# A middle stage in groups of four tiles: centred contexts, gathers ahead, inverse roots on ScalarE

## The reference, cut to what matters

```python
x = x + cross_attention_16_heads(layernorm(x), ctx)     # first stage
x = x + ffn_16_experts_capacity_256(layernorm(x))       # expert loop; its gather ends in the middle stage
# third layer (middle stage): ctx is 77 x 128 per tile, used as key and as value
scores = einsum('bqd,bkd->bqk', layernorm(x), ctx) * 128 ** -0.5
scores = where(tril, scores, -inf)
x = x + einsum('bqk,bkd->bqd', softmax(scores), ctx)
# fourth layer (product-key stage) starts from layernorm(x)
x = x + product_key_experts(layernorm(x)) + dense(layernorm(x))

def layernorm(x): return (x - mean(x)) / sqrt(var(x) + 1e-5)
```

## Time and profile before

| | us |
|---|---|
| median of three runs (lowest, highest) | 562.79 (561.74, 563.52) |
| the profiled execution's own time | 563.48 |
| its span, first to last instruction | 561.6 |
| VectorE's last copy of the expert loop starts | 182.49 |
| first maxima of the product-key stage start | 276.47 |
| first weighing on GpSimd (L485) starts | 292.48 |
| busy over the span: PE, DVE, ACT, POOL | 415.8, 387.1, 336.9, 357.5 |

### The profile page before, as it was taken

One profiled execution on the slowest core, in us unless ns is written; L12 is line 12 of the kernel. 1 busy time (PEld: TensorE's weight loads), 2 busy tenths in 40 slices (PEclk: granted clock), 3 DMA queues, 4 the chain that ended last, 5 costly groups with the idle time before them and its releaser, 6 DMA issues.

```text
span 561.6 us, 9520 instructions
## 1 busy us (share of the span) xinstructions
PE 415.8 (74%) x2518; PEld 347.8 (62%) x2518; DVE 387.1 (69%) x1668; ACT 336.9 (60%) x614; POOL 357.5 (64%) x256
## 2 busy tenths in 40 slices
PE   4959877169999034768857787888897778779864
PEld 2757766148999024657636675777676556667754
DVE  3558767102232125977789999999999999999980
ACT  2354553211222033565448888899888899888885
POOL 5227777710000547742249988888988888998883
PEclk9788698559999555555768999888989999998899
DMA  7980001016663101100000000000000000000000
GB/s 204 323 228 25 24 29 39 28 57 195 195 195 107 44 23 38 39 28 0 4 6 11 20 14 14 19 9 19 19 19 9 19 9 19 19 19 9 19 5 15
DMA packets 42415, 29.68 MB, mean 53 GB/s; under 512 B 4155, under 2 KB 38555, under 8 KB 42395
## 3 DMA queue, kind: packets, MB, share of 16 engines
q1 hardware_dynamic: 38539, 22.85, 13.9%
q0 software_dynamic: 2624, 6.30, 3.3%
q10 hardware_dynamic: 1232, 0.31, 0.3%
HBM read 18.95 MB, written 8.39 MB: 49 GB/s over the span
## 4 chain that ended last, share of the span: by engine, by line
DVE 23%; POOL 20%; PE 16%; ACT 12%; issue 7%; DMA 2%; POOLq 1%; DVEq 1%; ACTq 0%; SPq 0%
POOL arena_sb L485 13%; DVE picked_sb L1346 9%; ACT arena_sb L680 6%; PE bank L880 6%; PE bank L890 5%; ACT L680 3%; POOL yg_sb L448 3%; DVE bank L1308 2%; DVE first_sb L1305 2%; POOL slots L416 1%; PE bank L934 1%; POOL rstd_sb L366 1%; DVE bn_sb L1052 1%; DVE best_sb L1334 1%; POOLq L79 1%
## 5 line engine op out<-in xcount | busy, mean ns | idle before, releaser
L485 POOL TENSOR_TENSOR arena_sb<-arena_sb,picked_sb 128x2192 f32<-128x2192 f32 x32 | 154.4, 4847 | 30.8 <-DVE picked_sb L1346 23.7
L1346 DVE SCALAR_TENSOR_TENSOR picked_sb<-arena_sb,best_sb,bank 128x36 f32<-128x36 f32 (+1 forms) x256 | 107.8, 494 | 1.2
L990 PE MATMUL bank<-ident_sb,arena_sb 128*128 128x128 f32 (+1 forms) x512 | 71.8, 300 | 36.0 <-DVE arena_sb L1359 33.0
L990 PEld LDWEIGHTS bank<-ident_sb,arena_sb 128*128 128x128 f32 (+1 forms) x512 | 65.2, 166 | 41.2 <-issue 28.9
L477 POOL TENSOR_TENSOR arena_sb<-near_sb,sim_y_sb 128x1536 f32<-128x1536 f32 x32 | 87.7, 2762 | 1.4 <-DVE near_sb L1313 1.4
L680 ACT ACTIVATE arena_sb<-arena_sb,bsum_sb 128x548 f32<-128x548 f32 x128 | 85.7, 740 | 1.2 <-POOL arena_sb L485 0.8
L674 ACT ACTIVATE arena_sb<-arena_sb 128x2192 f32<-128x2192 f32 x32 | 65.3, 2041 | 0.2
L511 ACT ACTIVATE xn_sb<-x_all_sb,nb_sb,rstd_sb 128x128 f32<-128x128 f32 (+1 forms) x64 | 25.5, 480 | 38.2 <-POOL nb_sb L367 29.9
L981 PE MATMUL bank<-w_down_t_sb,h_sb 128*128 128x128 f32 x256 | 35.6, 284 | 15.8 <-DVE x_all_sb L1365 15.1
L445 POOL CAST made_row_sb<-gather_row_sb 128x4 uint32<-128x4 f32 (+1 forms) x8 | 1.5, 188 | 71.2 <-DMA made<-arena_sb 70.8
L981 PEld LDWEIGHTS bank<-w_down_t_sb,h_sb 128*128 128x128 f32 x256 | 32.0, 196 | 19.3 <-issue 19.3
(11 more groups left out here) (167 smaller groups left out, 928.1 us busy)
## 6 DMA issues: line engine op xcount, KB each, us to landing
w_sb<-w SPq DMA_DIRECT2D x32, 256.0 KB, 3.2
x_all_sb<-x SPq DMA_DIRECT2D x8, 256.0 KB, 2.9
slots<-arena_sb POOLq DMA_DIRECT2D x4, 512.0 KB, 8.3
arena_sb<-slots SPq DMA_DIRECT2D x16, 128.0 KB, 3.0
made<-arena_sb SPq DMA_DIRECT2D x16, 128.0 KB, 1.9
xt_sb<-x_t_sb SPq DMA_DIRECT2D x32, 64.0 KB, 1.8
out<-x_all_sb SPq DMA_DIRECT2D x32, 64.0 KB, 1.6
ctx_t_sb<-ctx_t SPq DMA_DIRECT2D x8, 154.0 KB, 3.6
```

Source lines behind the costliest of these rows:

```text
L485: pool.tensor_tensor(pp[p][:, :, :], pp[p][:, :, :], picked[p][:, :, :], ALU.mult).then_inc(weighed, 1)
L990: ins = pe.matmul(bank[4 * p][0:n, c * P:(c + 1) * P], pp[p][:, h, c * P:c * P + n], ident[:, :], is_transpose=True, start=h == 0, stop=h ...
L1346: ins = dve.scalar_tensor_tensor(out=picked[p][:, h, lo:hi], in0=vv[p][:, h, lo:hi], scalar=best[p][:, h, TOP - 1:TOP], in1=scores, op0=AL ...
```

## The change

The middle stage is unrolled and goes by groups of four tiles instead of pairs of groups; every small buffer of it has two copies, one per parity of the group.

1. Gathers: one cast turns all 32 columns of row numbers into integers, right behind the last scatter. The gathers go to `made_x`, a buffer for all 32 tiles laid over the memory of `picked`. Sixteen are issued at once, then four behind the small operations (`biases3`) of each of the groups 0 to 3.
2. Centring: the transposed contexts are multiplied with a centring matrix (identity less 1/128) in five matmuls of up to 512 columns between the first stage and the expert loop, and ScalarE copies the results over `ctx_t`. A token's mean then adds nothing to its scores, so the raw tile is transposed, and its inverse deviation becomes the scale of the exponential. ScalarE's normalisation ahead of the scores is gone, and the maximum is taken of unscaled scores and multiplied by the scale afterwards (`biases`).
3. Roots: ScalarE computes the inverse root as exp(-1/2 ln(v + eps)), for the second norm of 128 v, which takes in the factor 128 ** -0.5. A set of activation functions is named ahead of the stage.
4. The normalisation for the last stage moves from VectorE to ScalarE, with its bias made by GpSimd from the root.
5. The last group is finished inside the start of the product-key stage: ScalarE's `roots3`, `last_tokens` and `last_tokens_out` stand between `similarities(0, 1)` and `hidden(0, 0)`, TensorE's `last_tokens_t` behind `up(FIRST, 1)`. VectorE has nothing of it.
6. Transposed last tokens use the banks of the attended values; TensorE waits for the last maximum ahead of the first keys. SyncE's first `load_d` waits for one group's tokens, not for a pair's.

```diff
+            pool.tensor_copy(made_row[:, :], gather_row[:, :]).then_inc(made_row_ready, 1)
+            def gathers(g):
+                for n in range(g * BT, g * BT + BT):
+                    pool.indirect_dma_start(out=made_x[:, n, :], out_offset=None, in_=a["made"],
+                                            in_offset=bass.IndirectOffsetOnAxis(ap=made_row[:, n:n + 1], axis=0)
+                                            ).then_inc(gathered[g], 16)
+            def biases3(g):
+                p = g % 2
+                pool.wait_ge(croot3_ready, g + 1)
+                if g >= 2:
+                    pool.wait_ge(cxh_ready, g - 1)
+                step(pool.tensor_tensor(cnb[p][:, :], cmv3[p][:, :, 0], crstd[p][:, :], ALU.mult))
+                pool.tensor_scalar(cnb[p][:, :], cnb[p][:, :], -1.0, None, ALU.mult).then_inc(crstd3_ready, 1)
...
+            hold(pool, made_row_ready, 1)
+            gathers(0)
+            gathers(1)
+            gathers(2)
+            gathers(3)
+            for g in range(NB):
+                biases3(g)
+                if g + 4 < NB:
+                    gathers(g + 4)
```

ScalarE, centring and the middle stage:

```diff
+            for n, (lo, hi) in enumerate(pieces):
+                act.wait_ge(cc_mm, n + 1)
+                copy(cc_ready, ctx_row[:, lo:hi], bank[(0, 2, 3, 4, 6)[n]][:, 0:hi - lo])
...
+            def roots2(g):
+                p = g % 2
+                act.wait_ge(cstat2_ready, g + 1)
+                step(act.activation(cve2[p][:, :], cmv2[p][:, :, 1], ACT.Ln, bias=eps_d[:, 0:1], scale=float(D)))
+                if g >= 2:
+                    act.wait_ge(cbias_ready, g - 1)
+                act.activation(cscale[p][:, :], cve2[p][:, :], ACT.Exp, scale=-0.5).then_inc(crstd2_ready, 1)
...
+            def exps(g):
...
+                for t in range(BT):
+                    ins = act.activation(sc[p][:, t, :], sc[p][:, t, :], ACT.Exp, bias=cbias[p][:, t:t + 1],
+                                         scale=cscale[p][:, t:t + 1], accum_out=csum[p][:, t:t + 1])
...
+            act.preload_act_table_set("natural_log_exp_and_others")
+            tokens_out(0)
+            roots2(0)
+            exps(0)
+            tokens_out(1)
+            probabilities_out(0)
+            roots2(1)
+            exps(1)
+            tokens_out(2)
+            probabilities_out(1)
+            for g in range(NB - 2):
+                roots3(g)
+                roots2(g + 2)
+                last_tokens(g)
+                exps(g + 2)
+                if g + 3 < NB:
+                    tokens_out(g + 3)
+                last_tokens_out(g)
+                probabilities_out(g + 2)
+            roots3(NB - 2)
+            last_tokens(NB - 2)
+            last_tokens_out(NB - 2)
```

TensorE and VectorE, the orders (`tile(n)` is a raw tile of `x_all`):

```diff
+            for n, (lo, hi) in enumerate(pieces):
+                pe.matmul(bank[(0, 2, 3, 4, 6)[n]][:, 0:hi - lo], centre[:, :], ctx_row[:, lo:hi],
+                          start=True, stop=True).then_inc(cc_mm, 1)
...
+            for g in range(NB - 1):
+                attention(g)
+                if g:
+                    last_tokens_t(g - 1)
+                if g + 2 < NB:
+                    tokens_t(g + 2)
+                probabilities_t(g + 1)
+                if g + 2 < NB:
+                    scores(g + 2)
+            attention(NB - 1)
+            last_tokens_t(NB - 2)
...
+            for g in range(2, NB):
+                combine(g)
+                add_attention(g - 2)
+                statistics3(g - 2)
+                statistics2(g)
+                shares(g - 1)
+                maximum(g)
+                biases(g)
+            add_attention(NB - 2)
+            statistics3(NB - 2)
+            shares(NB - 1)
+            add_attention(NB - 1)
+            statistics3(NB - 1)
```

More of the change, by code:

```diff
@@ L230, in program @@
         stored = [sem(f"stored{p}") for p in two]
+        ctx_row = ctx_t[:, :, :].rearrange("p n k -> p (n k)")
+        pieces = [(lo, min(lo + 512, NT * TK)) for lo in range(0, NT * TK, 512)]
         block = ctx.enter_context(nc.Block())
@@ L1281, in turn @@
-            def turn(i, j, more):
-                step.turn()
-                for p in two:
-                    if more:
-                        combine(i + 1, p)
-                    maximum(i, p)
-                if more:
-                    combined_statistics(i + 1)
-                if j is not None:
-                    last_tokens(j)
-                add_attention(i)
-            for p in two:
-                combine(0, p)
-            combined_statistics(0)
-            turn(0, None, True)
@@ L1297, in _, with tile, combine @@
-            with dve.Fori(1, NI - 1) as i:
-                turn(i, i - 1, True)
-            turn(NI - 1, NI - 2, False)
+            def tile(n):
+                return x_all[:, n, :]
+            def combine(g):
+                dve.wait_ge(gathered[g], 16 * BT)
+                for n in range(g * BT, g * BT + BT):
+                    ins = dve.scalar_tensor_tensor(out=tile(n), in0=made_x[:, n, :], scalar=gate[:, n:n + 1],
+                                                   in1=tile(n), op0=ALU.mult, op1=ALU.add)
+                ins.then_inc(x2_ready, 1)
@@ new lines, in _ @@
+            step.turn()
+            combine(0)
+            statistics2(0)
+            maximum(0)
+            biases(0)
+            combine(1)
+            statistics2(1)
+            shares(0)
+            maximum(1)
+            biases(1)
+            for g in range(2, NB):
[6 more added lines that the diff above has]
+                biases(g)
@@ L1400, in _ @@
             own_sums(0, 1)
-            turn(0, None, True, before_picks=stage_c_last)
+            turn(0, None, True)
             with dve.Fori(1, NT // 2 - 1) as i:
```

346 lines of the change are left out of this document (157 added, 189 removed).

## The result

The changed kernel takes **533.49 us** (median of four runs, 533.03 to 534.30) against 563.15 for the kernel before (four runs, 561.74 to 568.69): a ratio of 0.9457, 95% interval 0.9393 to 0.9522. The forecast was 532.7 us in a range of 529.0 to 543.0. The profiled execution took 534.30 us with a span of 532.6; before it was 563.48 with 561.6.

A forecast was written before the change was run, and what follows sets the result against it. Bound taken: no full engine, but the order in which pairs of four-tile groups walk through the engines. First weighing 30.1 us earlier takes 563.48 to 533.4; the median, 0.7 lower, gives 532.7 us, range 529.0 to 543.0.

The forecast's parts named there:

- Opening: Start of the middle stage: one early cast puts the first gather at 185.5 us, group 0's bias at 198.0.
- Cadence: Middle stage, time per group: 6.8 us while TensorE's clock is low, then 6.3 bound by VectorE, against 8.3 before.
- Clock: TensorE in the middle stage: rises from 1.2 GHz at about 215 us once its pauses end; VectorE then bounds.
- rival 1: TensorE's clock stays at 1.2 GHz: groups 3 to 7 cost 6.8 us each, tail 1.4 more, 536.1 us; chance 0.24.
- Tail: From group 7's bias at 242.6 us: first maxima at 251.3, first weighing at 262.4, 30.1 earlier than before.
- Moves costed at nothing: Centring, new table load, constants, token loads, TensorE's new wait and the moved normalisation: hidden or already counted, no added time.
- Rival 2: GpSimd's queue: gathers wait behind an earlier group's bias in a two-group loop of 11.6 us plus queueing; 541.2 us, chance 0.16.
- rival 3: ScalarE: tables reloaded for every logarithm and exponential, four loads per group, 11.8 us per group; 571 us, slower, chance 0.05.
- Rival 4: Middle stage: groups still walk one by one at 8.3 us, only opening and tail gain; 544.7 us, chance 0.07.
- Last stage: Behind the first weighing: its period stays unchanged, so whatever brings that weighing forward comes off the time.

The follow-up runs named there:

- e5: Changed kernel with four further statistics instructions, results unused, on VectorE in each of groups 2 to 7: 537.63 us.
- e6: Changed kernel with eight more identity transposes on TensorE behind the attention of groups 0 to 6: 534.13 us.
- e8: e7 with ten more transposes behind the first scores and four to eight behind the attention of every group but the last: 533.04 us.
- e7: Changed kernel with 84 identity transposes on TensorE between the last expert matmul and the middle stage's first transposes: 533.72 us.
- e3: Changed kernel without the matmuls and copies that centre the contexts, that part of the computation left out: 534.14 us.
- e4: Changed kernel with the last group's normalisation moved from ScalarE to VectorE, ahead of its first picks: 540.76 us.
- e2: Changed kernel with gathers issued three groups ahead, not four: 558.72 us.
- e1: Changed kernel without the line naming one activation set for logarithm and exponential: 569.28 us.
- e11: Changed kernel with first keys multiplied around group 7's attention and both wide exponentials ahead of the hidden values' activations: 536.73 us.
- e12: e11 with eight identity transposes behind the attended values of groups 1 to 6: 536.28 us.
- e9: Kernel before the change with only the single cast of all row numbers added, GpSimd's loop unrolled for it: 559.97 us against 563.83.
- e10: Changed kernel with both roots back on GpSimd as powers of four values: 542.40 us.

## Why the prediction was right

The mechanism is the one forecast, and the total is 0.8 us off. That is better than the terms deserve: the middle distance was forecast at 79.9 (262.4 less 182.49) and is 81.19, 1.3 longer, all of it in the tail, and the expert loop, whose last copy happened to start 0.89 earlier, covered most of it. That part is luck.

- **Opening.** First gather forecast at 185.5, measured 184.71. Behind the last expert copy that is 3.01 forecast (185.5 less 182.49) and 3.11 measured: of the 0.44 that was taken 0.34 came. First bias 15.51 behind that copy by forecast and 15.57 measured.
- **Cadence.** From the first bias to the last 44.6 us were forecast (198.0 to 242.6) and 44.39 measured. The terms hold: exponentials 438 ns for 348, 90 more, as worked out from the three rows; a root 0.52 with its gap, for 0.55; the table load at 178.70, inside idle time. VectorE as the bound is shown by e5, with a reserve: 0.84 of dose cost 0.77 against the steps at the high clock, and 0.46 against the mean of all.
- **Clock.** A rise at about 215 was forecast and came, at about 213.6, was gone again from 218 to 220, and came back (0.99 in 222 to 231). **One step that failed** is "then VectorE bounds: the bias of group 3 at 217.3, groups 4 to 7 at 6.3 each", as far as it let the clock stay up: with 0.07 us of work in 1 it fell behind 217, and with 4.95 in 9 at 231. Group 4 took 6.48, groups 6 and 7 took 6.66 and 6.63, near rival 1's 6.8. The working looked for TensorE's pauses to end at 1.2 GHz and did not ask how many come back at 2.4. At the high clock the steps are 6.04 (e6 as well), shorter than the 6.3 forecast, so the mean came out right from two errors. The price of the whole question is small: e6 to e8 held the clock up in different stretches and moved the middle distance by -0.4, 0.0 and +1.7.
- **Tail.** From the last bias to the first weighing 19.8 was forecast, 21.2 measured; to the first maxima 8.7 and 10.21. **The other step that failed**, with the larger error, is here. From the last bias to the roots of group 6 the sum has 4.6 and the trace 3.88, since the roots stand behind the copy of the probabilities and don't wait for the attended values. Roots and normalisation took 2.79, 2.8 in the sum. From there to the first maxima the sum leaves 1.3 us (250.0 to 251.3), which its transposes and its copy fill but for 0.1, so that the keys' matmul and two extracts are in it by name only. Measured are 3.54 (248.23 to 251.77): 0.14 to the transposes, 0.88 until the keys follow in TensorE's queue, 1.95 for the keys and 0.57 for the extracts; the copy runs beside them. Of these 3.54 some 1.3 are the low clock, by an estimate from rows at the high one (0.47 for such transposes at 223.18, 1.10 for the keys), so 1.0 is missing at either clock. Rival 1 priced its tail at 21.2; that the figure fits exactly is luck, though its low clock was there up to 251. The add of group 7 waits 3.32 us for attended values at 1.2 GHz, but it is off the path: VectorE is idle for another 1.10 behind it, until ScalarE's extract. From the maxima to the weighing 11.1 was forecast and 11.02 measured. ScalarE's first wide exponential ended at 262.47 (261.8), the picks at 262.64 (262.4): two paths within 0.2 us. In e6 and e7 the first maxima came 1.37 and 0.79 earlier behind the last expert copy, which is VectorE's path; ScalarE's ended only 0.16 earlier and 0.25 later, with TensorE's clock lower in the tail than in the changed kernel. This is why they gained next to nothing.
- **Moves costed at nothing.** The centring is hidden (e3). TensorE's part was two instructions of 0.64 us per piece, 1.28 in sum, near the estimate of 1.2. Finishing group 7 on ScalarE is worth 5.8 (e4), not the 3.00 us of VectorE's work alone.
- **Rivals.** Rival 2's loop was forecast at 11.6 and is 11.45 (e2); rival 3's step at 11.8 and is 11.48, its time at 571 and is 569.3 (e1). Rival 4 fell with the cadence. Rival 1 came true for two groups of eight, for part of a third, and in the tail up to 251.
- **Last stage.** Period forecast unchanged: 16.63 and 16.64 from weighing to weighing, and 16.64 before. The 0.69 us more behind the first weighing comes at the very end: behind the start of the last one (512.35, and 542.62 before) the span runs 20.25 us for 18.98. TensorE's clock there is 0.50 from 522 to 526, where it was 1.00 from 550 to 560 in the kernel before, and its last 32 transposes are busy 6.73 us for 3.94. In the other profiles the stretch from the first weighing took 268.51 to 270.54 with the last stage's code the same (e11 and e12 aside), so it can't be laid to the change.

What of the gain belongs to which edit can be said only for single ones, each added alone or taken back alone: the casts 3.7 (e9), roots off GpSimd 9.9 (e10), a depth of four against three 25 (533.5 and 558.7, e2). They overlap, since each is the bound once the others are gone, and their sum is no total. Whether moving the first normalisation off the path, by centred contexts, would have gained anything without the new order was not tried.

## What to carry to other kernels

When a stage is bound by no engine but by the order in which work passes through several, cost each engine's work per step and also every loop that comes back to a queue (here combine, statistics, root, bias, gather, landing): divided by the number of steps that it spans, it is the bound or it isn't, and one more step ahead was worth 25 us here. When two functions of ScalarE alternate, see from the table loads in the trace that one loaded set serves both. At a seam between stages look at the second turn, not only at the first event: e11 brought the first weighing 2.3 us forward and the second one 2.5 us back.

## What was not expected of the hardware

- TensorE's clock fell in the middle of steady work once the higher clock had made room for pauses: 8.64 us busy of 9 ahead of the rise, 4.95 of 9 at 0.99, then 0.50. The Trainium skill ("TensorE: Matmul & The Clock Gate", Part 1) says that activity releases the throttle; the trace agrees, and shows the way back as well. Eight idle transposes per group were enough to keep it at 0.97 (e6). Which stretch has the high clock counts: e6 won up to 1.4 us ahead of the first maxima and lost 1.0 behind them.
- The first gather behind a wait starts about 0.7 us later than a cast in its place does (3.12 against 2.39 us behind the last expert copy). Where it has not waited the idle time ahead of it is 0.17 to 0.30.
- A gather usually lands 2.5 us after its issue, but the last one of group 6 took about 3.4 in the changed kernel (issued at 225.36, combined at 228.74) and 4.2 in e8. VectorE's waits for that group, 0.30 and 1.12, come from it.
- The last copy of the same expert loop started anywhere within 3.2 us in the profiles of this study (180.35 to 183.49). Without the distance measured from it, several of the verdicts above would have been lost in that.
